# Attention output projected to token rows and summed onto the residual, in a two-layer block on one core

## The reference

```python
x = hidden                                     # (1, 2048, 128)
h = layernorm(x)
q, k, v = h @ w_q, h @ w_k, h @ w_v            # 16 heads of 64
scores = einsum('bqhd,bkhd->bhqk', q, k) * 64**-0.5 + dilated_mask(2048)
attn = softmax(scores)
x = x + einsum('bhqk,bkhd->bqhd', attn, v).reshape(1, 2048, 1024) @ w_o
z = fp4_quant_dequant(layernorm(x))            # blocks of 16
x = x + fp4_linear(silu(fp4_linear(z, w_gate)) * fp4_linear(z, w_up), w_down)
...                                            # recurrent mixer, MLP, channel mix: not touched
```

## Time and profile before

| | us |
|---|---|
| median of 3 executions | 470.29 |
| lowest, highest | 467.96, 470.34 |
| span of the profiled execution, first to last instruction | 468.2 |
| PE busy | 443.3 (95%) |
| DVE busy | 394.1 (84%) |
| ACT busy | 333.0 (71%) |
| POOL busy | 296.5 (63%) |

### The profile page before, as it was taken

One profiled execution on the slowest core, in us unless ns is written; L12 is line 12 of the kernel. 1 busy time (PEld: TensorE's weight loads), 2 busy tenths in 40 slices (PEclk: granted clock), 3 DMA queues, 4 the chain that ended last, 5 costly groups with the idle time before them and its releaser, 6 DMA issues.

```text
span 468.2 us, 17264 instructions
## 1 busy us (share of the span) xinstructions
PE 443.3 (95%) x6440; PEld 348.8 (74%) x6440; DVE 394.1 (84%) x1344; ACT 333.0 (71%) x975; POOL 296.5 (63%) x491
## 2 busy tenths in 40 slices
PE   7999699999999999999999899998987989999996
PEld 5687588888888888888787678887744757558775
DVE  5888598997988899799797697996899989998775
ACT  3678668778768777877786678695566579987533
POOL 4222576687576768667865587665669897674322
PEclk9999999999999999999999999999999999999999
DMA  6477952356345335445455564464000000000003
GB/s 224 175 254 201 276 122 53 75 115 123 75 84 110 74 74 109 81 78 109 86 116 122 110 135 90 77 123 91 1 1 0 0 2 0 2 0 2 1 0 91
DMA packets 136098, 40.53 MB, mean 87 GB/s; under 512 B 104976, under 2 KB 131024, under 8 KB 136016
## 3 DMA queue, kind: packets, MB, share of 16 engines
q1 hardware_dynamic: 135440, 38.38, 35.9%
q10 hardware_dynamic: 576, 1.05, 0.6%
HBM read 29.44 MB, written 9.96 MB: 84 GB/s over the span
## 4 chain that ended last, share of the span: by engine, by line
PE 59%; POOL 9%; DMA 8%; DVE 8%; ACT 7%; SPq 4%; issue 3%; ACTq 0%; POOLq 0%; DVEq 0%
PE psum L464 10%; PE psum L422 10%; PE psum L484 5%; PE psum L1186 5%; PE psum L498 5%; PE psum L495 4%; PE psum L510 4%; PE psum L403 4%; DMA st<-w_rows_dram 3%; DMA w_rows_dram<-st 3%; PE psum L1181 3%; ACT pband L569 3%; PE psum L405 2%; PE psum L404 2%; POOL area L1827 2%
## 5 line engine op out<-in xcount | busy, mean ns | idle before, releaser
L948 POOL TENSOR_SCALAR pband<-pband,fac 128x192 f32<-128x192 f32 x256 | 103.9, 424 | 84.8 <-DVE fac L771 84.7
L569 ACT ACTIVATE pband<-pband,st 128x192 f32<-128x192 f32 x256 | 113.2, 448 | 0.9 <-DVE st L719 0.9
L719 DVE CUSTOM_DVE_ANT_0 pband<-psum,band_mask 128x192 f32<-128x192 f32 x256 | 76.0, 353 | 0.1
L422 PE MATMUL psum<-keys,q_class 64*64 64x192 f32 (+2 forms) x1536 | 66.3, 274 | 0.0
L464 PEld LDWEIGHTS psum<-ident,pband 128*128 128x128 f32 x384 | 45.3, 141 | 25.5 <-issue 17.8
L464 PE MATMUL psum<-ident,pband 128*128 128x128 f32 x384 | 53.1, 273 | 6.1 <-DVE arena L836 3.1
L422 PEld LDWEIGHTS psum<-keys,q_class 64*64 64x64 f32 x1536 | 57.7, 133 | 1.4 <-issue 1.4
L569 ACT ACTIVATION_READ_ACCUMULATOR pband<-pband,st 128x1 f32 x256 | 49.5, 193 | 0.0
L938 POOL COPY q_class<-q_rows 128x512 f32<-128x512 f32 x32 | 36.4, 1137 | 14.0 <-ACT q_rows L609 14.0
L930 POOL COPY keys<-k_rows 128x512 f32<-128x512 f32 x32 | 36.2, 1131 | 14.3 <-issue 7.2
L780 DVE COPY pt<-psum 128x512 f32<-128x512 f32 x64 | 43.6, 682 | 0.4
(11 more groups left out here) (213 smaller groups left out, 1086.4 us busy)
## 6 DMA issues: line engine op xcount, KB each, us to landing
v_rows_dram<-arena SPq DMA_DIRECT2D x32, 256.0 KB, 4.6
v_both<-v_rows_dram SPq DMA_DIRECT2D x32, 256.0 KB, 3.9
v_seg<-v_rows_dram SPq DMA_DIRECT2D x64, 128.0 KB, 3.8
v_side<-v_rows_dram SPq DMA_DIRECT2D x96, 64.0 KB, 2.6
w_rows_dram<-st SPq DMA_DIRECT2D x64, 8.0 KB, 3.0
st<-w_rows_dram SPq DMA_DIRECT2D x64, 8.0 KB, 2.5
arena<-_attn_hidden_states_dram SPq DMA_DIRECT2D x4, 256.0 KB, 3.9
out_dram<-x SPq DMA_DIRECT2D x4, 256.0 KB, 2.5
```

Source lines behind the costliest of these rows:

```text
L422: return pe.matmul(bank[2 * r + head][rows, at:at + y.shape[1]], x, y, start=True, stop=True, skip_group_check=True)
L569: act.activation(x, x, ACT.Exp, bias=mine[:, head:head + 1], scale=-1.0, accum_out=mine[:, 2 + head:3 + head]).then_inc(s_exp, 1)
L719: dve.tensor_tensor_reduce(pband[:, G % P_SLOTS, c, head, :], bank[2 * r + head][:, at:at + BAND], band_mask[:, (0, 1, 1, 2)[w], SEG * (1 ...
L948: pool.tensor_scalar(x, x, fac[:, F % 2, 1, c, head:head + 1], 1.0, ALU.mult, ALU.mult).then_inc(s_scaled, 1)
```

## The change

The output projection swaps its operands. `o_sb` becomes the stationary operand, in four tiles of 128 tokens, and `wo` streams past it: four products of 128 columns, each giving 128 tokens by 128 features. Bank 7 then has the layout of `x_rows`, and `accumulate(U)` adds it to `x_rows[U % 4]` directly. The first four sums no longer copy but add, and so wait for the loaded token rows (`s_load`). The loads move ahead: `x_rows[0]` behind the fetch of step 3, the others at the end of steps 4, 5 and 6 (ROW_STEP is 4). `acc`, `t1` and `x1` are gone; the waits that `t1` made for others stand at `t2` and `qx6`. `x_rows` moves to the place of `acc`.

```diff
-    RAW_STEP, QUANT_STEP, ROW_STEP, PLAIN_STEP = 6, 12, 20, 22
+    RAW_STEP, QUANT_STEP, ROW_STEP, PLAIN_STEP = 6, 12, 4, 22
...
+            def load_x_rows(g):
+
+                sp.wait_ge(s_vst[g], 16 * len(range(g, V_TILES, V_SLOTS)))
+                load_rows(sp, hidden, x_rows[g], s_load[g], g)
...
             fetch_statistics(2); load_sides(0, 3); load_wo(); send_statistics(3); fetch_statistics(3)
+            load_x_rows(0)
...
-                if F == ROW_STEP:
-                    for w in range(NW):
-                        stored(1, w)
-                if ROW_STEP <= F < ROW_STEP + NG:
-                    g = F - ROW_STEP
-                    load_rows(sp, hidden, x_rows[g], s_load[g], g)
+                if ROW_STEP <= F < ROW_STEP + NG - 1:
+                    load_x_rows(F - ROW_STEP + 1)
...
-                pe.matmul(shared_bank[:, :], wo[:, U // NW, :], o_sb[:, :], start=True, stop=True).then_inc(s_mix, 1)
+                for a in range(TW):
+                    tile = slice(P * a, P * (a + 1))
+                    last = pe.matmul(shared_bank[:, tile], o_sb[:, tile], wo[:, U // NW, :], start=True, stop=True,
+                                     skip_group_check=True)
+                last.then_inc(s_mix, 1)
...
-                cols = acc[:, U % NW * WT:(U % NW + 1) * WT]
+                rows = x_rows[U % NW][:, :, :].rearrange("p a d -> p (a d)")
                 dve.wait_ge(s_mix, U + 1)
                 if U < NW:
-                    dve.wait_ge(s_vst[U], 16 * len(range(U, V_TILES, V_SLOTS)))
-                    dve.tensor_copy(cols, shared_bank[:, :]).then_inc(s_acc, 1)
+                    dve.wait_ge(s_load[U], 16)
                 else:
                     dve.wait_ge(s_acc, U - NW + 1)
-                    dve.tensor_tensor(cols, shared_bank[:, :], cols, ALU.add).then_inc(s_acc, 1)
+                dve.tensor_tensor(rows, shared_bank[:, :], rows, ALU.add).then_inc(s_acc, 1)
...
-        def t1(g):
-            pe.wait_ge(s_acc, NS_ALL - NW + g + 1)
-            if g == 1:
-                pe.wait_ge(s_weight, WEIGHT_TURNS)
-            if g == 2:
-                for odd in range(2):
-                    pe.wait_ge(s_pt[odd], 2 * NS_ALL)
-            if g == 3:
-                pe.wait_ge(s_out, NS_ALL)
-            transposes(g, lambda a: acc[:, GW * g + P * a:GW * g + P * (a + 1)], 0)
...
-        def x1(g):
-            wait_for(dve, "t1", g)
-            dve.wait_ge(s_load[g], 16)
-            end(dve.tensor_tensor(flat(x_rows[g]), flat(x_rows[g]), bk(g, 0)[:, :], ALU.add), g, "vector")
...
         def bn0(g):
-            wait_for(dve, "x1", g)
+            dve.wait_ge(s_acc, NS_ALL - NW + g + 1)
             moments(g)
```

More of the change, by code:

```diff
@@ L109, in attention @@
 def attention(nc, ctx, hidden, w_q, w_k, w_v, w_o, w_gate, w_up, w_down, plain_weights, columns, ident, constants,
-              x_rows, s_load, v_rows, scratch, acc, arena, grid, natural, psum, out):
+              x_rows, s_load, v_rows, scratch, arena, grid, natural, psum, out):
     def sb(name, shape, dt=F32):
@@ L255, in attention @@
         nc, lambda name, shape, dt=F32: ctx.enter_context(nc.sbuf_tensor(name, shape, dt)), sem, psum, bank, ident, constants,
-        x_rows, s_load, grid, natural, acc, out, s_acc, s_max, s_seg, s_quant, s_plain, s_pt, s_out)
+        x_rows, grid, natural, out, s_acc, s_max, s_seg, s_quant, s_plain, s_pt, s_out)
     with nc.Block() as block:
@@ L545, in _ @@
             weigh(28, 2); weigh(28, 3); turn_weights(0); turn_weights(1); turn(29, 0); output(28); turn_weights(2)
-            turn(29, 2); turn(29, 1); t1(0); turn_weights(3); turn_weights(4); turn(29, 3); turn_weights(5)
+            turn(29, 2); turn(29, 1); turn_weights(3); turn_weights(4); turn(29, 3); turn_weights(5)
             weigh(29, 0); weigh(29, 1); weigh(29, 2); weigh(29, 3); turn_weights(6); turn(30, 0); turn(30, 1)
-            output(29); turn_weights(7); turn(30, 3); turn(30, 2); weigh(30, 0); weigh(30, 1); t1(1); weigh(30, 2)
-            weigh(30, 3); turn(31, 1); t2(0); turn(31, 0); turn(31, 3); output(30); turn(31, 2); gu0(0); t1(2)
-            weigh(31, 0); weigh(31, 1); weigh(31, 2); weigh(31, 3); gu1(0); output(31); t2(1); t1(3); gu2(0); gu0(1)
+            output(29); turn_weights(7); turn(30, 3); turn(30, 2); weigh(30, 0); weigh(30, 1); weigh(30, 2)
+            weigh(30, 3); turn(31, 1); t2(0); turn(31, 0); turn(31, 3); output(30); turn(31, 2); gu0(0);
+            weigh(31, 0); weigh(31, 1); weigh(31, 2); weigh(31, 3); gu1(0); output(31); t2(1); gu2(0); gu0(1)
             gu3(0); gu1(1); t2(2); gu2(1); gu0(2); gu1(2); t2(3); gu3(1); gu0(3); gu2(2); t3a(0); gu1(3); t3b(0)
@@ L836, in take_values, with zero_pads @@
                 dve.tensor_copy(v_slot(i), turn_bank[i % 2][:, :]).then_inc(s_vev[i % 2], 1)
+            def zero_pads():
+                dve.wait_ge(s_wlo, 4)
+                dve.memset(raw[P - R:P, 0:2, 2 * P:FT], 0.0)
+                dve.memset(raw[:, 2, FF:FT], 0.0).then_inc(s_zero, 1)
             def blocks(x):
@@ L903, in _ @@
             even_turned(28, 2); band_max(31, 1); accumulate(27); seg_sums(31); differences(30); clear()
-            even_turned(29, 0); accumulate(28); factors(30); x1(0); bn0(0); ag0(0); even_turned(29, 2)
+            even_turned(29, 0); accumulate(28); factors(30); bn0(0); ag0(0); even_turned(29, 2)
             differences(31); qx0(0); qx1(0); qx2(0); even_turned(30, 0); factors(31); accumulate(29)
-            even_turned(30, 2); qx7(0); qx8(0); x1(1); xq(0); bn0(1); ag0(1); even_turned(31, 0); xqt(0)
-            accumulate(30); even_turned(31, 2); qx0(1); qx2(1); x1(2); hm0(0); bn0(2); ag0(2); qx7(1); qx8(1); hm1(0)
-            accumulate(31); qa0(0); qx0(2); x1(3); qx2(2); bn0(3); hm2(0); ag0(3); qa2(0); qx7(2); hm0(1); qx8(2)
+            even_turned(30, 2); qx7(0); qx8(0); xq(0); bn0(1); ag0(1); even_turned(31, 0); xqt(0)
+            accumulate(30); even_turned(31, 2); qx0(1); qx2(1); hm0(0); bn0(2); ag0(2); qx7(1); qx8(1); hm1(0)
+            accumulate(31); qa0(0); qx0(2); qx2(2); bn0(3); hm2(0); ag0(3); qa2(0); qx7(2); hm0(1); qx8(2)
             hm3(0); qb0(0); qx0(3); hm1(1); qx2(3); qa0(1); qb2(0); qa7(0); qx7(3); qx8(3); hm0(2); qa2(1); hm2(1)
@@ L1069, in wait, with tokenwise @@
         eng.wait_ge(s, value)
-def tokenwise(nc, sb, sem, psum, bank, ident, c, x_rows, s_load, grid, natural, acc, out, s_acc, s_max, s_seg, s_quant, s_plain,
+def tokenwise(nc, sb, sem, psum, bank, ident, c, x_rows, grid, natural, out, s_acc, s_max, s_seg, s_quant, s_plain,
               s_pt, s_out):
@@ L1369, in qx6 @@
         def qx6(g):
+            if g == 0:
+                act.wait_ge(s_max, 8 * NS_ALL)
+                act.wait_ge(s_seg, 2 * NS_ALL)
+            if g == 1:
+                act.wait_ge(s_weight, WEIGHT_TURNS)
+            if g == 2:
+                act.wait_ge(s_pt[0], 2 * NS_ALL)
+            if g == 3:
+                act.wait_ge(s_out, NS_ALL)
             binades(g, "x", "qx4")
@@ L1953, in two_layers @@
         arena = sb("arena", [P, 6016 + PLAIN * P])
-        acc = arena[:, 0:T]
-        x_rows = [arena[:, T + GT * D * g:T + GT * D * (g + 1)].rearrange("p (a d) -> p a d", d=D) for g in range(NG)]
+        x_rows = [arena[:, GT * D * g:GT * D * (g + 1)].rearrange("p (a d) -> p a d", d=D) for g in range(NG)]
         natural = arena[:, 6016:6016 + PLAIN * P].rearrange("p (t d) -> p t d", d=P)
@@ L1959, in two_layers @@
                   (in_proj, out_proj, fc, proj, w_r, w_kk, w_vv), (norm1, norm2, mu_r, mu_k), ident, c,
-                  x_rows, s_load, v_rows, w_rows.rearrange("p x -> (p x)"), acc, arena, grid, natural, psum, out)
+                  x_rows, s_load, v_rows, w_rows.rearrange("p x -> (p x)"), arena, grid, natural, psum, out)
 _INS = ["L0_attn_hidden_states", "L0_attn_w_q", "L0_attn_w_k", "L0_attn_w_v", "L0_attn_w_o", "L0_ffn_w_gate",
```

17 lines of the change are left out of this document (9 added, 8 removed), and 16 rows, old and new, of the table STEPS.

## The result

The changed kernel takes **472.5 us** (median of 20 runs, 469.53 to 478.31) against 469.62 us of the kernel before (20 runs, 467.6 to 472.95): a ratio of 1.0066, with a 95% interval of 1.0042 to 1.0089, so it is slower by 3.1 us. The forecast was 474.3. The changed kernel also spreads wider, over 8.8 us against 5.4.

What follows compares the result with a forecast made beforehand. PE was taken to bound the attention, busy through ordinary iterations of 9.26 or 8.79 us. The terms 6.4 + 1.0 - 2.2 - 1.2 = +4.0 us on 470.29 gave 474.3 us, 8-in-10 range 469.3 to 478.8.

Steps and rivals of the forecast that it cites:

- rivals A and B: A: DVE's room hides all the loads, 467.9 us, chance 0.09; B: only the first load is felt, 470.1 us, chance 0.20.
- late loads hold the first sums: Early attention: sums wait for token rows loaded late in SP's queue, delaying query projections; +6.4 us, bounds 3.5 to 8.8.
- short products: Output projection: eight passes take 0.89 us against 0.86, +0.03 us a step, +1.0 us over 32 steps, bounds 0 to 1.3.
- loads leave steps 20 to 23: Late attention: the two long iterations lose their excess once the token-row loads move; -2.2 us, between 0 and -2.7.
- groups start without `t1`, `x1`: End of the attention: without these, `rs0(3)` and all behind it move earlier; -1.2 us, between -0.6 and -2.7.
- SP ends the fetch of step 3 at 71.03 + 1.29 = 72.32: SP's queue: the time load 0 is issued, so it lands at 76.3 and the first sum starts then, not at 72.12.
- the path that was drawn: Late loads delay sums, DVE's `differences` and SP's sending; query projections come 2.2, 4.3 and finally 6.4 us late, each containing earlier delays.
- three places foreseen: PE idle 2 us before the query projections of iterations 7, 9 and 10.
- The landings: Token-row loads take 3.0 to 5.1 us to land; the median, 3.9, was used for each moved load.
- rival C: Output projection: weight loads of short products not covered, eight at 192 ns, +0.68 us a step, 22 us, 496 us; chance 0.03.
- The 81 ns for a product of 128 columns: Skill's figure against the change: eight short products 386 ns dearer than two long, +12 us over 32 steps; earlier rows disagreed.
- the upper bound: Steps 20 to 23: the whole excess there, 0.74 + 1.92 = 2.7 us, goes.

Runs made afterwards that it cites:

- loads sooner: The changed kernel with the load of x_rows[0] issued ahead of the fetch of step 3 and the other three right behind it: 468.42 us, ratio 0.9989.
- loads behind the fetch: The changed kernel with loads 1 to 3 issued right behind the statistics' fetch, ahead of the step's side loads: 469.65 us, ratio 0.999.
- step 14: The kernel before with the token-row loads at steps 14 to 17: 468.08 us, ratio 0.9959; with the output product also cut into four: 468.07 us, 0.9988.
- loads moved alone: The kernel before with only the token-row loads moved to the change's places, awaited only in the second half: 467.94 us, ratio 0.9971.
- step 10: The kernel before with the token-row loads at steps 10 to 13 in place of 20 to 23: 468.14 us, ratio 0.9978.
- changed, once more: The changed kernel run again, nothing edited: 472.01 us, ratio 1.0068 to the kernel before.
- idle turns back: The changed kernel with the four transposes t1 and four additions x1 put back as idle work, same order and waits: 475.33 us, ratio 1.0102.
- eight short products: The kernel before with the output product cut into eight products of 64 columns instead of one of 512: 492.06 us, ratio 1.0461.

## Why the prediction was right, and where it was off

The time, the sign and the mechanism came out as forecast, and rivals A and B fell: the loads are not hidden, and not only the first is felt. That the sum came so near owes something to chance: three of its four terms were too large in size, and their errors partly cancel. The terms, as the ratios of the experiments give them against 469.3 us, each uncertain by 1 to 2 us:

| term | forecast, us | measured, us | from |
|---|---|---|---|
| late loads hold the first sums | +6.4 | +3.6 | changed kernel against loads sooner and loads behind the fetch |
| short products | +1.0 | +0.9 (+2.6 when first measured, alone) | step 14 with and without them |
| loads leave steps 20 to 23 | -2.2 | -1.4 | loads moved alone, at step 14, at step 10 |
| groups start without `t1`, `x1` | -1.2 | -0.1 | loads sooner with and without them |
| sum | +4.0 | +3.0 | changed kernel measured directly: +3.1 |

With 2.6 for the short products the sum would be +4.7, so the agreement of 3.0 and 3.1 proves less than it seems to.

**The start.** The step that was off is "SP ends the fetch of step 3 at 71.03 + 1.29 = 72.32". It was read from one execution and carried as if it were the kernel's. That fetch ended 4.28 us behind the start of step 1 on PE there; over 13 profiled executions of all these kernels it ended between 1.1 and 5.7 us behind it, six times below 2. Load 0 hangs on it, and then the place of everything behind:

| profiled execution | load 0 issued | DVE's wait at sums 0, 2, 3 | PE, start of step 0 to start of step 5 |
|---|---|---|---|
| before | - | - | 44.06 |
| changed | 68.83 | 1.26, 4.28, 0.73 | 47.29 |
| changed, once more | 72.78 | 5.63, 3.83, 1.28 | 50.86 |
| idle turns back | 70.05 | 1.14, 2.57, 4.83 | 51.74 |
| loads behind the fetch | 70.33 | 1.56, 0, 0.56 | 45.92 |
| loads sooner | 65.74 | 0, 0, 0 | 44.21 |

Kernels whose first sums wait for no load show 44.06 to 45.13 in that last column (eight short products left aside). Against it the three stalled executions lose 2.2 to 3.2, 5.7 to 6.8 and 6.6 to 7.7 us, so the forecast's 6.4 is what a bad execution pays, inside the bounds of 3.5 to 8.8; over all executions it is 3.6. And the 6.4 is not reached by the path that was drawn. PE's waits for these sums come to 2.0, 4.3 and 4.6 us in the three. In the third the low clock adds 2.7, for which the forecast had no term. The mean granted clock of single executions hints how often: it is below 0.991 in 8 of 38 executions of the two kernels that stall, and in none of the 189 others that have it on record. At 2.7 us each that would be 0.6 us of the mean, an estimate. The sums named as waiting (first, third, fourth, and not the second) are the ones that wait, and PE stood at each of the three places foreseen, but never at all three in one execution: iteration 7 and 9, or 9 and 10, or 9 alone. That the delays do not add but contain one another held: in the changed kernel's second trace 10.7 us of waits on DVE cost PE about 6. That a late first sum delays SP's sending of step 5 shows only there (18.7 us behind the start of step 1, against 14.5 before); where the first wait was 1.1 to 1.6 us, the sending was not late. The same wandering of SP's place, with the clock that can follow, is what I take for the wider spread of the changed kernel; that was argued from three traces, not tested.

**The landings** were 2.9 to 5.5 us, median 3.6, against 3.0 to 5.1 with a median of 3.9; this carried over.

**The short products** take 0.89 us as worked out from the earlier trace rows, 0.03 more a step, and rival C fell for the length in the change. One halving further on, at 64 columns, 22.5 us are lost. That this is its very 22 is chance: it priced eight loads at 192 ns from the earlier trace rows, which is how long one load lasts, where the trace has sixteen passes, each with a load, that follow every 0.112 us while the loads overlap. That it is the load which sets this floor fits the records, where loads and passes start equally far apart, but no run with fewer stationary columns tests it. The Trainium skill, "TensorE: Matmul & The Clock Gate", section "LDWEIGHTS (loading the stationary operand)", gives a load as its columns over 1.2, so 107 ns for 128 columns; the trace nearly agrees, with 112. The 81 ns for a product of 128 columns, of the section "Back-to-back issue gap", which the prediction set aside, no run here shows for 128 stationary columns of this type: with 128, 64 and 16 moving columns the passes start 0.11 us apart.

**Steps 20 to 23.** In the trace the whole 2.6 us went, as the upper bound had it, and another 0.3 in steps 23 and 24 (8.94 and 8.91 us before, 8.79 now with the loads moved alone), which the forecast did not count. The time shows 1.4. What hides the rest may be the start: steps 0 and 1 together take 17.2 to 17.5 us on PE in four of the traces and 17.8 to 18.2 in seven (eight short products and the changed kernel's second trace left aside). In four of the seven the granted clock reads 0.50 for the first 1.3 to 1.9 us of step 0, after 2.1 to 3.2 us in which PE was idle. In the other three PE waits 0.5 to 0.8 us in step 1 for the load of `wo`. The trace before had neither.

**The start of the groups.** The step that failed is that VectorE's time there was on the path for 1.2 us. What became shorter in every trace is the stretch behind step 31, by 0.3 us; the times of steps 23 to 30 together overlap, 67.5 to 69.0 us without `t1` and `x1` and 68.2 to 68.7 with them (four short products in both). Ahead of it the last `differences` waits for the statistics anyway: 0.9 to 1.4 us in the traces with `t1`, `x1` and the long product, 2.2 to 2.9 with four short products, 3.4 to 3.8 with these and without `t1` and `x1`. What DVE saved became a longer wait for the same DMA.

**A version better than both.** The kernel before with the loads at step 14: 0.9959. With the runs at step 10 and at steps 3 to 6 it makes three that lie 0.2 to 0.4% below the kernel before; their intervals overlap, so none of the three places is shown to be best. The changed design with loads that come in time (0.9989 and 0.999) shows no gain over that, as its products cost about 1 us and its savings at the tail give next to nothing.

## What to carry to other kernels

When an accumulator starts from data in memory instead of from a copy, its load gets a deadline: put it in the queue ahead of anything small that can wait, and ahead of the fetch that the same engine waits for next. A load without a deadline can be tried at another step: this one number gave 1.4 us here, the whole rearrangement none. Read a queue's place from several executions before you build a sum on it. Look in the trace you have for the shortest pass of the same type before you cut a matmul shorter. And when you price a wait of TensorE, look at its clock behind the wait too.

## What was not expected of the hardware

- A pass of fp32 with 128 stationary columns has a floor: 0.112 us from start to start with 128 moving columns, with 64 and with 16, though the same pass with 512 takes 0.43. Between 128 and 64 columns the cost of cutting a product goes from 0.03 us a step to 0.87.
- One wait of PE of 3.44 us came with 6.9 us at the 1.2 GHz level and cost 6.1 us in all; a sum of waits alone had no place for the other 2.7.
- The place of one queue entry against PE moves by 4.6 us over 13 executions of programs that are all but the same up to there, and a small DMA's turn (the statistics written, then read back) goes with it: where the landing of the written ones is on record, the fetch begins 0.01 to 0.02 us behind it.
- A load of 256 KB that stood right behind four side loads landed in 5.5, 5.3, 5.0 and 3.9 us in the four traces that have it so; the load before it, behind a fetch, landed in 2.8 to 2.9 us in all four.
